# High and low part of the turned probabilities through one 512-column matmul, added on VectorE

## What is computed

```python
q = q.reshape(B, S, NUM_HEADS, HEAD_DIM)          # 1 x 2048 x 16 x 128
scores = jnp.einsum('bqhd,bkhd->bhqk', q, k) / jnp.sqrt(jnp.float32(HEAD_DIM))
attn = jax.nn.softmax(scores, axis=-1)
out = jnp.einsum('bhqk,bkhd->bqhd', attn, v).reshape(B, S, NUM_HEADS * HEAD_DIM)
return _mxfp4_matmul(out, wo_codes, wo_scales) + bo
```

## Time and profile before

| | |
|---|---|
| Times of three runs | 2112.35, 2115.59, 2116.29 us |
| Median | 2115.59 us |
| Span of the profiled execution, first to last instruction | 2115.3 us |
| TensorE matmuls, busy | 2049.6 us, 97% |
| TensorE weight loads, busy (beside matmuls) | 1866.8 us, 88% |
| VectorE, busy | 1730.4 us, 82% |
| GpSimd, busy | 1548.8 us, 73% |
| ScalarE, busy | 1410.8 us, 67% |

### The profile page before, as it was taken

How to read it: one execution, slowest core, us unless ns; L and a number is a source line. 1 busy time by engine, 2 the same in 40 slices (tenths; PEclk the granted TensorE clock), 3 DMA queues, 4 the chain that set the end, 5 groups by cost and what they waited for, 6 DMA issues and landing times.

```text
span 2115.3 us, 36713 instructions
## 1 busy us (share of the span) xinstructions
PE 2049.6 (97%) x13236; PEld 1866.8 (88%) x13236; DVE 1730.4 (82%) x2523; ACT 1410.8 (67%) x2575; POOL 1548.8 (73%) x1329
## 2 busy tenths in 40 slices
PE   7999999999999999999999999999999999949998
PEld 5899999999999999999999999899989999838887
DVE  6888878988989888988888898888888888865553
ACT  5777767776777667776677677766777677625343
POOL 2679778886879777877797787877787678846333
PEclk9999999999999999999999999999999999969999
DMA  4667657776667666766676666766676567740000
GB/s 99 155 156 178 158 139 163 170 164 158 146 160 175 151 149 153 181 155 140 162 174 161 148 155 155 179 147 150 153 170 154 136 161 165 161 121 1 11 11 21
DMA packets 216599, 298.50 MB, mean 141 GB/s; under 512 B 44897, under 2 KB 85345, under 8 KB 216417
## 3 DMA queue, kind: packets, MB, share of 16 engines
q1 hardware_dynamic: 216416, 296.15, 59.8%
HBM read 25.46 MB, written 2.10 MB: 13 GB/s over the span
## 4 chain that ended last, share of the span: by engine, by line
PE 84%; SPq 5%; POOL 3%; DVE 3%; ACT 2%; DMA 1%; issue 1%; POOLq 0%; DVEq 0%; ACTq 0%
PE ps_s L497 14%; PE ps_s L498 14%; PE ps_s L499 14%; PE ps_a L499 12%; PE ps_a L498 12%; PE ps_a L497 12%; SPq L316 4%; POOL pT_lo L409 3%; ACT probs L819 1%; PE ps_a L749 1%; PE ps_a L752 1%; PE ps_a L751 1%; DMA pT<-probs 1%; DVE part_max L1065 1%; PE ps_s L735 0%
## 5 line engine op out<-in xcount | busy, mean ns | idle before, releaser
L409 POOL TENSOR_TENSOR pT_lo<-pT,pT_hi 128x512 fp32r<-128x512 f32 x1024 | 1302.8, 1302 | 358.6 <-ACT pT_hi L832 357.6
L832 ACT ACTIVATE pT_hi<-pT 128x512 fp32r<-128x512 f32 x1024 | 612.4, 628 | 232.6 <-DMA pT<-probs 163.5
L819 ACT ACTIVATE probs<-ps_s,shift 128x1024 f32<-128x1024 f32 x512 | 566.6, 1109 | 223.3 <-DVE shift L1074 223.0
L1065 DVE TENSOR_REDUCE part_max<-ps_s 128x1 f32<-128x1024 f32 x512 | 622.0, 1217 | 67.5 <-PE ps_s L499 65.8
L1084 DVE STREAM_TRANSPOSE probs<-probs 128x1024 f32<-128x1024 f32 x512 | 619.4, 1229 | 65.4 <-ACT probs L819 64.6
L497 PE MATMUL ps_a<-pT_hi,v_hi 128*128 128x256 f32 x2048 | 578.7, 283 | 1.5 <-POOL pT_lo L409 1.4
L499 PE MATMUL ps_a<-pT_hi,v_lo 128*128 128x256 f32 x2048 | 579.9, 283 | 0.0
L498 PE MATMUL ps_a<-pT_lo,v_hi 128*128 128x256 f32 x2048 | 579.7, 283 | 0.0
L497 PE MATMUL ps_s<-kT_hi,qT_hi 128*128 128x512 f32 x1024 | 405.2, 396 | 11.7 <-ACT probs L819 8.5
L497 PEld LDWEIGHTS ps_a<-pT_hi,v_hi 128*128 128x128 f32 x2048 | 391.8, 191 | 19.0 <-POOL pT_lo L409 2.5
L498 PEld LDWEIGHTS ps_a<-pT_lo,v_hi 128*128 128x128 f32 x2048 | 391.8, 191 | 15.5
(11 more groups left out here) (160 smaller groups left out, 2917.5 us busy)
## 6 DMA issues: line engine op xcount, KB each, us to landing
pT<-probs SPq DMA_DIRECT2D x2048, 128.0 KB, 2.5
pT<-in_L_attn_x SPq DMA_DIRECT2D x4, 512.0 KB, 5.7
codes<-in_L_attn_wk_codes SPq DMA_DIRECT2D x16, 128.0 KB, 2.4
scales<-in_L_attn_wk_scales SPq DMA_DIRECT2D x64, 32.0 KB, 3.0
codes<-in_L_attn_wo_codes SPq DMA_DIRECT2D x16, 128.0 KB, 2.3
scales<-in_L_attn_wo_scales SPq DMA_DIRECT2D x64, 32.0 KB, 1.9
x<-in_L_attn_x SPq DMA_DIRECT2D x4, 512.0 KB, 7.1
layer_out<-x SPq DMA_DIRECT2D x8, 256.0 KB, 2.1
```

Of the source, the lines that this page charges most:

```text
L409: pool.tensor_tensor(pT_lo[:, p, :].rearrange("p (i n) -> p i n", i=Q4), pT[:, s % 2, g, :, t:t + 2, :].rearrange("p i t q -> p i (t q)"), ...
L819: nc.scalar.activation(out, src, ACT.Exp, bias=shift[:, s % SLOTS, r:r + 1], scale=SCALE, accum_out=sums[:, s % SLOTS, r, g:g + 1])\
L832: nc.scalar.activation(pT_hi[:, p, :].rearrange("p (i n) -> p i n", i=Q4), pT[:, s % 2, g, :, t:t + 2, :].rearrange("p i t q -> p i (t q)" ...
L1065: V.tensor_reduce(part_max[:, s % SLOTS, r, g:g + 1], ring_of("s", w, NG2 * r + g), AX.X, ALU.max)\
```

## The change

The two parts of the turned probabilities lie in one tile, `pT_both`, side by side for each ring place; `pT_hi` and `pT_lo` are views of it. The first two matmuls of each value product, which have the same stationary operand `v_hi`, become one of 512 columns: the product with the high part goes to columns 0 to 255 of the bank, as before, and that with the low part to columns 256 to 511. The third matmul (`v_lo` x high) is as before. The two halves of the bank are added on VectorE, within the step that makes the low part: first left half minus `oT_hi` into a new tile `oT_rest`, then right half plus `oT_rest` into `oT_lo`. A semaphore `out_rest` stands between the two. `oT_hi` on ScalarE still comes from the left half alone.

```diff
-        pT_hi = sb("pT_hi", [P, RING, 2 * HQ], f32r, att)
-        pT_lo = sb("pT_lo", [P, RING, 2 * HQ], f32r, att)
+        pT_both = sb("pT_both", [P, RING, 2, 2 * HQ], f32r, att)
+        pT_hi, pT_lo = pT_both[:, :, 0, :], pT_both[:, :, 1, :]
         oT_hi = sb("oT_hi", [P, HQ], f32r, att)
         oT_lo = sb("oT_lo", [P, HQ], f32r, att)
+        oT_rest = sb("oT_rest", [P, HQ], f32, att)
...
                 out = ps_a[:, s % 2, 0:HQ].rearrange("p (i q) -> p i q", i=Q4)
-                hi = pT_hi[:, p, :].rearrange("p (i t q) -> p i t q", i=Q4, t=2)
-                lo = pT_lo[:, p, :].rearrange("p (i t q) -> p i t q", i=Q4, t=2)
+                out_both = ps_a[:, s % 2, :].rearrange("p (b i q) -> p b i q", b=2, i=Q4)
+                both = pT_both[:, p].rearrange("p b (i t q) -> p b i t q", i=Q4, t=2)
                 for t in range(2):
                     k = 2 * p + t
-                    last = product3(out, v_hi[:, k, h % 2, :], v_lo[:, k, h % 2, :], hi[:, :, t, :], lo[:, :, t, :],
-                                    first=k == 0, last=k == KT - 1)
+                    nc.tensor.matmul(out_both, v_hi[:, k, h % 2, :], both[:, :, :, t, :], start=k == 0, stop=False)
+                    last = nc.tensor.matmul(out, v_lo[:, k, h % 2, :], both[:, 0, :, t, :], start=False,
+                                            stop=k == KT - 1)
                 last.then_inc(sm["pv_done"], 1)
...
                 wait(dve, "out_hi", w + 1)
-                V.tensor_tensor(oT_lo[:, :].rearrange("p (r i q) -> p i r q", r=RH, i=Q4),
+                V.tensor_tensor(oT_rest[:, :].rearrange("p (r i q) -> p i r q", r=RH, i=Q4),
                                 ps_a[:, s % 2, 0:HQ].rearrange("p (i r q) -> p i r q", r=RH, i=Q4),
                                 full(oT_hi[:, :]).rearrange("p (r i q) -> p i r q", r=RH, i=Q4), ALU.subtract)\
+                    .then_inc(sm["out_rest"], 1)
+                wait(dve, "out_rest", w + 1)
+                V.tensor_tensor(oT_lo[:, :].rearrange("p (r i q) -> p i r q", r=RH, i=Q4),
+                                ps_a[:, s % 2, HQ:2 * HQ].rearrange("p (i r q) -> p i r q", r=RH, i=Q4),
+                                oT_rest[:, :].rearrange("p (r i q) -> p i r q", r=RH, i=Q4), ALU.add)\
                     .then_inc(sm["out_lo"], 1)
```

More of the change, by code:

```diff
@@ L162, in sandwich_layer @@
             xn_done xn_t xT_hi_done xT_lo_done
-            scores_ready max_part shift_ready p_ready p_turned p_hi_done p_lo_done pv_done out_hi out_lo
+            scores_ready max_part shift_ready p_ready p_turned p_hi_done p_lo_done pv_done out_hi out_rest out_lo
             total_done rinv_ready oproj_ready acc_done q_ready q_hi q_lo k_ready k_hi k_lo v_ready v_hi_done v_lo_done
```

## The result

The changed kernel takes 2106.57 us (median of eight runs, 2105.3 to 2110.09), the kernel before 2115.38 on the same chip (eight runs, 2112.35 to 2119.25). The ratio is 0.996, with an interval of 0.995 to 0.997. On another chip it was 0.9951 (0.9939 to 0.9964; 2106.36 against 2117.38). The forecast was 2107.3. The profiled execution has a span of 2104.5 us against 2115.3.

The account below looks back on a forecast made before the run. The prediction took TensorE's matmul issue in attention as the bound. Saving 14.1 us less 2.8, 2.6 and 0.4 given back leaves 8.3 us off the 2115.3 us span: 2107.0, or 2107.3 us as median time, range 2101 to 2117.

Parts of the forecast that it names:

- What bounds the kernel: In attention TensorE issues without a break, busy 500.00 of 500 us; other engines' work is free unless it reaches TensorE.
- The saving on TensorE, 14.1 us: Value matmuls: each removed one saves its fixed 0.0069 us, 2048 times, 14.1 us in all.
- d = 0.42 on VectorE: Output's low part: the second, dependent operation lengthens VectorE's slot from 0.31 to 0.73 us in each half.
- rival 3: GpSimd holds up VectorE's second operation, making the kernel slower, up to 137 us longer; chance 0.08.
- The loop of VectorE and ScalarE against TensorE: Per attention half, the loop grows to 12.55 us against TensorE's 12.59, so TensorE stays the bound by 0.04.
- Rival 1: VectorE's and ScalarE's loop becomes the bound in attention, giving 2110 to 2116 us; chance 0.15.
- No stall in the steady state: Output projection's room behind VectorE's low part falls from 0.75 to 0.28 us, so TensorE does not wait.
- (a): Every second head: a 40.2 us stretch set by SyncE's issue queue doesn't shrink, giving back 2.8 us over eight heads.
- (b): TensorE's five waits for an exponential, from late transfers, each grow by up to 0.53 us: 2.6 us given back.
- (c): End of attention: the output projection's last wait for the low part gives back 0.4 us, 1.3 if all three do.
- Rival 2: The joined value matmul saves between nothing and a third: 2112 to 2118 us, set at 2114; chance 0.20.
- The sum: Whole kernel: 14.1 - 2.8 - 2.6 - 0.4 = 8.3 us less, giving 2107.3 us, 0.4% faster.

Follow-up runs that it names:

- e1: The changed kernel with its second VectorE operation taken out, so only the joined matmul is kept and one product is left out: 2101.74 us, ratio 0.9932.
- e4: The changed kernel with a weight's scales loaded by one or two DMAs instead of four: 2110.32 us, ratio 0.9974.
- e5: The changed kernel with matmuls of two key blocks reordered to 512, 512, 256, 256 columns: 2099.1 us, ratio 0.9922.
- e2: The kernel before the change, its matmuls kept, with a second dependent VectorE operation for the output's low part: 2116.77 us, ratio 1.0002.
- e3: The changed kernel with the low part of the value bias (vb_lo) moved from VectorE to ScalarE: 2103.84 us, ratio 0.9941.
- e10: The kernel before the change, nothing joined, with four v_hi matmuls then two v_lo, all of 256 columns: 2116.08 us, ratio 0.9992.

## Point by point: why the prediction was right, and where not

- **What bounds the kernel.** Right. TensorE is the bound in attention, and the gain is read off its start-to-start times.
- **The saving on TensorE, 14.1 us.** The mechanism was right, the size not. The term was the fixed share of 0.0069 us for each removed matmul. Measured, a block went from 0.3584 to 0.3488 in the mean: 0.0096 us, or 20 us in all. By the halves, 0.14 us in the mean (the forecast was 0.11), it is 18. What failed is the step that took the spacings of 256 and of 512 columns, each among its like, and added them: the joined matmul costs 0.2329 as forecast (0.2325), but the 256-column one beside it 0.1166 and not 0.1197. The spacing depends on the neighbour, and the 0.113 us behind a score matmul stood in the trace of before. The Trainium skill (TensorE: Matmul & The Clock Gate, section "Back-to-back issue gap") has a fixed gap of about 2.5 ns in its formula for a single matmul, which by the forecast's estimate would have given 5.1 us. The matmul alone brought 14.7 in net time, so no run here agrees with it.
- **d = 0.42 on VectorE.** Right: 0.45. The second operation took 423 to 428 ns in all 128 halves, and rival 3 (GpSimd holds it up) is refuted. But the effect that rival 3 feared exists, on an operation it didn't name: the same engine's vb_lo, which reads and writes SBUF alone, took 0.28 us or up to 1.4.
- **The loop of VectorE and ScalarE against TensorE.** Right: plain halves take 12.54 to 12.58, forecast 12.59. ScalarE's wait for TensorE fell from 0.57 to 0.18, less far than to the 0.1 forecast. VectorE's maximum waits 0.16. Rival 1 did not come: the waits for exponentials stayed at 4.1 us.
- **"No stall in the steady state" of the output projection.** Wrong in even heads, and in the odd heads with a long vb_lo. In even heads the room fell from 0.75 not to 0.28 but to 0.06, and TensorE waited. The step took d and 0.05 for TensorE's gain off it. That gain took 0.08 (of the 0.21 that e1 shows, 0.13 are a longer vb_lo). Above all the step held all else on VectorE fixed, but vb_lo, a few operations ahead, takes 0.36 us more than before, 1.39 instead of 1.03. Cost: 8 x 0.30 = 2.4 us, and 0.7 to 1.0 us in an odd head whose vb_lo is long, two heads in after and five in its second execution (a sixth, behind the longest place 12, lost nothing). I had chosen the half with the least room, but hadn't asked which operation ahead of it has a length that depends on the moment.
- **(a) odd heads, 2.8 us.** The place is right, and the size can't be told well: by the medians place 12 takes 13.16 where 12.75 would be its share of the gain, 8 x 0.41 = 3.3 us; by the means it is 0.5 us in all, and 4.2 in the second execution. That TensorE's own pace brings the loss is borne out by e1, which has 13.66 there without the second operation. The mechanism was incomplete. I wrote that the stretch is SyncE's queue alone. That is so in the third odd head of after; in three others the chain also passes the landing of the scales and GpSimd's operations, and e4, which shortened the queue, left this one and won nothing.
- **(b) waits for exponentials, 2.6 us more.** Wrong: 4.3 us before, 4.1 after, 5.8 in the second execution.
- **(c) end of attention, 0.4 us.** Too small for the profiled execution: 1.9 us, above the bound of 1.3 that I gave. The second execution has 0.65, from before's last score matmul to last projection (35.11) to its own (35.76). The rest in after goes with a wait for GpSimd (1.96) that e1 and the second execution haven't got.
- **Rival 2, the joined matmul saves less.** Refuted; it saves more.
- **The sum.** Forecast: 14.1 - 5.8 = 8.3. Found: about 18 of gain, less 7 in places 2, 5 and 12 and 1.9 at the end, which makes 9; the profiled spans differ by 10.8, the medians by 8.8. That the forecast's time came out this close is luck: two errors met with opposite signs, 4 us too little gain, and 3 too little (9 against 5.8) of what eats it.

## What to carry to other kernels

Measure the cost of a matmul in the very pattern in which it will stand: its spacing changed with its neighbours. Grouping the equal lengths (e5) gave the fastest kernel here; how much of that is the order's and how much a shorter vb_lo's isn't settled. When the engine that bounds gets faster, go through all rooms on the others again, and of each ask which operations ahead of it vary in length: an addition of 0.43 us that is free at the old pace (e2) cost 4 to 6 us at the new one. Where an engine gets such an addition, look first for a small operation on that engine which an idle one can take (e3: 2.4 us in place 5 for one edit). And look at every head, and at a second execution of the same kernel, before a wait is put down to the change: place 12, place 13 and the end of attention differ between two executions of one kernel by about as much as the change moves them.

## What the runs showed of the hardware that I had not expected

- **Spacing of matmuls depends on order.** Alone among their like 256 columns take 0.1197 us and 512 take 0.2325. A pair of them takes 0.3488 in alternation and 0.3468 grouped (means over attention), both under the sum of 0.3522. A 256-column matmul takes 0.113 us directly behind a 512-column score matmul (before). With equal lengths grouping changes nothing (e10).
- **One VectorE operation from SBUF to SBUF takes 0.28 us or up to 1.4.** VectorE's vb_lo (128x128) has both lengths in after, and the two operations on the output, which have a PSUM operand, never left 377 to 428 ns. The extra 1.1 us is less than one of GpSimd's operations beside it (5.06 us for four, 1.27 each). Over the eleven executions with vb_lo on VectorE, 111 of its 176 instances are long (0.94 to 1.43 us), and every one of them ends 0.08 to 0.09 us behind the end of an operation of GpSimd's; the 65 short ones end 0.18 us or more behind one. So the end of a long one follows the end of the running operation, or of the next one. In the odd heads nearly every vb_lo starts 0.07 to 0.09 us before an operation of GpSimd's ends, and it is then sometimes short and sometimes as long as the whole next one. The Trainium skill (SBUF — State Buffer, section "SBUF: two separate sides") says that GpSimd and certain VectorE operations share a pair of ports, which the one that starts first locks for its whole instruction. The trace agrees as far as it goes; the lock itself no run here shows.
- **Fewer DMAs can land later.** From the start of issuing to the operation that waits, one broadcast of four rows to 128 partitions took 3.41 to 5.02 us (e4, ten heads in which GpSimd waits), four of one row each to 32 partitions 3.30 to 3.55 (after, nine heads), though the four take 1.83 us to issue and the one 0.60. Two heads of before, with four DMAs, took 4.71 and 5.28.
